# Wide cross-attention with its 64-channel heads: the given weights in place of folded ones

## The reference, cut to what matters

```python
xn, latn = _layernorm(x, ln1_w, ln1_b), _layernorm(latents, ln2_w, ln2_b)
q = latn @ Wq                                     # 16 heads of 64 channels
k, v = jnp.split(jnp.concatenate([xn, latn], axis=1) @ Wkv, 2, axis=-1)
...
weight = jax.nn.softmax(jnp.einsum('bhld,bhnd->bhln', q * scale, k * scale), axis=-1)
out = jnp.einsum('bhln,bhnd->bhld', weight, v)
return out.transpose(0, 2, 1, 3).reshape(b, l, INNER) @ Wo
```

## Time and profile before

| | us |
|---|---|
| median of 3 runs (2155.71 to 2158.64) | 2157.29 |
| the profiled execution, span | 2153.9 |
| PE busy | 1989.9 |
| DVE busy | 1582.0 |
| ACT busy | 1349.8 |
| POOL busy | 1015.9 |

### The profile page before, as it was taken

The page is one execution under the profiler, slowest core; times in us unless marked ns, Lnnn a source line. Parts: engine busy times, 40 slices in busy tenths (PEclk is TensorE's granted clock), DMA queues, the critical chain, the costliest instruction groups (busy, mean ns, idle before and its releaser), DMA issues.

```text
span 2153.9 us, 44630 instructions
## 1 busy us (share of the span) xinstructions
PE 1989.9 (92%) x14787; PEld 1692.3 (79%) x14849; DVE 1582.0 (73%) x3470; ACT 1349.8 (63%) x3140; POOL 1015.9 (47%) x1222
## 2 busy tenths in 40 slices
PE   6999989999999999998049999999999999999998
PEld 4787789999999999984047888887677777777776
DVE  5668568888888888777775666676787777788775
ACT  4666556666666666666774666787655555555554
POOL 3555444444454445420003655554356666566665
PEclk9999999999999999998568999999899999999999
DMA  6433400000000000000004444455233333333342
GB/s 182 122 118 119 112 1 2 1 1 2 1 2 1 2 1 2 1 1 1 0 3 130 118 119 115 122 163 158 81 118 120 121 125 118 120 120 122 120 126 97
DMA packets 138908, 161.03 MB, mean 75 GB/s; under 512 B 15340, under 2 KB 99244, under 8 KB 138284
## 3 DMA queue, kind: packets, MB, share of 16 engines
q1 hardware_dynamic: 132524, 153.46, 23.9%
q10 hardware_dynamic: 6160, 4.78, 0.7%
HBM read 119.75 MB, written 38.70 MB: 74 GB/s over the span
## 4 chain that ended last, share of the span: by engine, by line
PE 67%; issue 9%; POOL 8%; DVE 5%; ACT 5%; SPq 3%; DMA 2%; ACTq 0%; POOLq 0%; DVEq 0%
PE bank L947 8%; POOL h_lo L2122 7%; PE bank L273 6%; PE bank L911 5%; PE bank L913 5%; PE bank L912 5%; PE bank L1777 5%; PE bank L958 5%; PE bank L1779 5%; PE bank L1778 5%; PE bank L284 3%; PE bank L255 3%; PE bank L1680 2%; PE bank L254 2%; SPq L191 1%
## 5 line engine op out<-in xcount | busy, mean ns | idle before, releaser
L2122 POOL TENSOR_TENSOR h_lo<-h,h_hi 128x512 fp32r<-128x512 f32 x264 | 341.2, 1293 | 244.7 <-ACT h_hi L1903 244.6
L1304 POOL TENSOR_TENSOR pw<-ew,rw 128x410 f32<-128x410 f32 x256 | 225.6, 881 | 368.2 <-DVE rw L1166 351.5
L556 DVE TENSOR_REDUCE nmx<-bank 128x4 fp32r<-128x512 f32 (+1 forms) x384 | 237.6, 620 | 192.3 <-PE bank L255 189.0
L449 ACT ACTIVATE pt<-bank 128x512 f32<-128x512 f32 (+1 forms) x384 | 229.1, 600 | 128.2 <-PE bank L273 127.1
L1896 ACT ACTIVATE sl<-bank 128x512 f32<-128x512 f32 x264 | 157.8, 598 | 237.9 <-PE bank L1779 236.5
L1067 ACT ACTIVATE ew<-bank,nmax 128x205 f32<-128x205 f32 x512 | 216.8, 431 | 132.7 <-DVE nmax L1158 132.7
L2041 DVE TENSOR_TENSOR bank<-bank,sl 128x512 f32<-128x512 f32 x264 | 184.1, 697 | 142.1 <-PE bank L1779 114.1
L706 POOL TENSOR_SCALAR_AFFINE_SELECT pt<-pt 128x512 f32<-128x512 f32 x256 | 162.3, 635 | 187.7 <-ACT pt L449 187.6
L273 PE MATMUL bank<-q_pack,k_diag 128*128 128x128 f32 (+1 forms) x1536 | 237.8, 279 | 0.3
L273 PEld LDWEIGHTS bank<-q_pack,k_diag 128*128 128x128 f32 (+1 forms) x1536 | 189.1, 181 | 46.2 <-issue 37.9
L947 PE MATMUL bank<-kvt,qs 128*128 128x205 f32 x1024 | 221.6, 339 | 0.0
(11 more groups left out here) (349 smaller groups left out, 5215.8 us busy)
## 6 DMA issues: line engine op xcount, KB each, us to landing
share_b<-share_rows SPq DMA_DIRECT2D x256, 256.0 KB, 3.1
q_rows<-q_hi SPq DMA_DIRECT2D x96, 128.0 KB, 2.7
q_pack<-q_rows SPq DMA_DIRECT2D x32, 384.0 KB
raw<-in_experts SPq DMA_DIRECT2D x33, 192.0 KB, 3.2
q_rows<-q_lo SPq DMA_DIRECT2D x48, 128.0 KB, 2.8
k_diag<-k_rows SPq DMA_DIRECT2D x64, 96.0 KB
q_pack<-q_rows SPq DMA_DIRECT2D x31, 192.0 KB
k_diag<-k_rows SPq DMA_DIRECT2D x124, 48.0 KB
```

What stands on the lines that cost most here:

```text
L449: nc.scalar.activation(m.pt[0:a.keys, c, :, :].rearrange("p h t -> p (h t)"), m.flip[c % 2][0:a.keys, :], ACT.Exp).then_inc(s.exped.semaph ...
L556: nc.vector.tensor_reduce(m.nmx[:, b % 2, :, 0, c], m.score[c % 2][:, 0:HC * a.columns].rearrange("p (h k) -> p h k", h=HC)[:, :, 0:a.keys ...
L1304: nc.gpsimd.tensor_tensor(m.pw[:, k, :, 0:KW], m.ew[:, k, :, :], m.rw[:, k, :].unsqueeze(2).broadcast_to([128, 2, KW]), ALU.mult)\
L2122: nc.gpsimd.tensor_tensor(m.h_lo[:, k % 3, :], m.h[:, (k + u) % 2, :], m.h_hi[:, k % 3, :].bitcast(F32), ALU.subtract).then_inc(s.los, 1)
```

## The change

The stage now computes queries, keys and values with the given weights. The products of weights are gone, `wide_w` holds Wq, Wk, Wv, Wo (128 x 1024 each) and is split once into `wide_hi` and `wide_lo`, in sequences 9 to 17 of attention 0; its four loads are issued at sequences 4 to 7 (before: 24 and 25). A couple of heads (2 x 64 channels) now fills 128 partitions:
- `query` and `key` make a couple's queries (256 columns) and keys (412 columns) for both sequences of the pair, with three products each, in odd steps, three couples ahead. DVE copies the queries and scales them, ACT copies the keys.
- `value` makes one of eight tiles of values in even steps: the values of half of the heads for one sequence and one part of its keys (128 or 77 rows), three products of 512 columns; DVE copies them to `vs`.
- `scores` are two fp32 products over 64 rows each: head 0 on rows 0 to 63, head 1 on rows 64 to 127, each into a bank of its own. Bank 0 serves head 0 of every step.
- `weigh` is four fp32 products (two parts of the keys by two heads), with 64 columns of weights and 128 moving columns; head h writes partitions 64 h to 64 h + 63. The probabilities aren't split any more, `pwt_lo` is gone.
- `project_out` is three products of 256 columns in even steps, where there were six in odd ones.
- The step's order on PE is scores, then the products of even or odd steps, then the transposes, then the weighing. The transposes share one bank (`turned`), both couples' mixes share another.
- POOL no longer splits the inputs: `kv_hi`, `kv_lo` are gone, and the split of the transposed inputs is on ACT and DVE.
- The start of the stage changes with it: transposed inputs at sequences 28 and 29, three value tiles, three keys and three queries up to the gap behind the last sequence.

The core of the diff:

```diff
-    def weight_products(g):
-        left, right = (0, 1) if g < 4 else (2, 3)
-        wait(pe, s.weight_lows, g)
-        for k in range(4):
-            h = 4 * (g % 4) + k
-            last = nc.tensor.matmul(m.products[:, 128 * k:128 * k + 128], m.wide_w[:, h, left, :],
-                                    m.wide_w[:, h, right, :], start=True, stop=True)
-        last.then_inc(s.weight_products, 1)
-
...
+    def value(p, v, t, bank, queries_before):
+        half, k, part = t // 4, t // 2 % 2, t % 2
+        wait(pe, s.queries, queries_before)
+        wait(pe, s.values, TILES * p + t)
+        pe.wait_ge(s.inputs_lo, 2 * p + k + 1)
+        rows = PART_ROWS[part]
+        keys, columns = slice(128 * part, 128 * part + rows), slice(512 * half, 512 * half + 512)
+        in_parts(bank[0:rows, :], m.kvt_hi[:, v, k, keys], m.kvt_lo[:, v, k, keys],
+                 m.wide_hi[:, WV, columns], m.wide_lo[:, WV, columns]).then_inc(s.valued, 1)
+
+    def query(p, v, c, bank, values_before):
+        wait(pe, s.values, values_before)
         wait(pe, s.queries, XC * p + c)
-        if c == 0:
-            pe.wait_ge(s.inputs_lo, p + 1)
-        for h in range(2):
-            last = in_parts(m.ask[:, 256 * h:256 * h + 256].rearrange("p (k t) -> p k t", k=2),
-                            m.score_hi[:, 2 * c + h, :], m.score_lo[:, 2 * c + h, :],
-                            m.kvt_hi[:, v, :, :], m.kvt_lo[:, v, :, :])
-        last.then_inc(s.asked, 1)
+        heads = slice(128 * c, 128 * c + 128)
+        in_parts(bank[:, 0:256].rearrange("p (k t) -> p k t", k=2), m.wide_hi[:, WQ, heads], m.wide_lo[:, WQ, heads],
+                 m.kvt_hi[:, v, :, 0:T], m.kvt_lo[:, v, :, 0:T]).then_inc(s.asked, 1)
+
+    def key(p, v, c):
+        wait(pe, s.keys, XC * p + c)
+        pe.wait_ge(s.inputs_lo, 2 * p + 2)
+        heads = slice(128 * c, 128 * c + 128)
+        in_parts(m.key_bank[:, 0:2 * KP].rearrange("p (k t) -> p k t", k=2), m.wide_hi[:, WK, heads], m.wide_lo[:, WK, heads],
+                 m.kvt_hi[:, v, :, 0:KP], m.kvt_lo[:, v, :, 0:KP]).then_inc(s.keyed, 1)
 
     def scores(p, v, n):
         j, c, k = STEPS * p + n, n // 2, n % 2
         pe.wait_ge(s.queries, XC * p + c + 1)
+        pe.wait_ge(s.keys, XC * p + c + 1)
         wait(pe, s.exped, j - 1)
+        wait(pe, s.exped_first, j)
         for h in range(2):
-            last = nc.tensor.matmul(m.score[k][:, KP * h:KP * h + KW], m.qs[:, c % 2, h, k, :],
-                                    m.kvt[:, v, k, 0:KW], start=True, stop=True)
+            rows = slice(XD * h, XD * h + XD)
+            last = nc.tensor.matmul(score_bank(m, k, h)[:, 0:KW], m.qs[rows, c % 2, k, :],
+                                    m.ks[rows, c % 2, k, 0:KW], start=True, stop=True)
         last.then_inc(s.scores, 1)
 
...
     def transpose_probs(p, v, n):
         j, k = STEPS * p + n, n % 2
         pe.wait_ge(s.probs, j + 1)
-        wait(pe, s.prob_lows, j - 1)
+        wait(pe, s.probs_s, j)
         for part in range(2):
             for h in range(2):
                 at = 256 * part + 128 * h
-                last = nc.tensor.transpose(m.flip[k][:, at:at + 128],
-                                           m.pw[:, k, h, 128 * part:128 * part + 128], m.ident[:])
+                last = nc.tensor.transpose(m.turned[0:PART_ROWS[part], at:at + 128],
+                                           m.pw[:, k, h, 128 * part:128 * part + PART_ROWS[part]], m.ident[:])
         last.then_inc(s.probs_t, 1)
 
     def weigh(p, v, n):
-        j, c, k = STEPS * p + n, n // 2, n % 2
-        if n == 0:
-            pe.wait_ge(s.contexts, 2 * p + 2)
+        j, c, k, half = STEPS * p + n, n // 2, n % 2, n // XC
+        pe.wait_ge(s.values, TILES * p + 4 * half + 2 * k + 2)
         if k == 0:
-            wait(pe, s.head_lows, XC * p + c - 1)
-        pe.wait_ge(s.prob_lows, j + 1)
+            wait(pe, s.head_lows, XC * p + c)
+        pe.wait_ge(s.probs_s, j + 1)
+        at = 256 * (c % 2) + 128 * k
         for part in range(2):
-            keys = slice(256 * part, 256 * part + 256)
-            last = in_parts(m.mix[c % 2][:, 256 * k:256 * k + 256], m.kv_hi[:, v, k, part, :], m.kv_lo[:, v, k, part, :],
-                            m.pwt_hi[:, k, keys], m.pwt_lo[:, k, keys], part == 0, part == 1)
+            rows = PART_ROWS[part]
+            for h in range(2):
+                head, probs = XD * (n // 2 % 4 * 2 + h), 256 * part + 128 * h
+                last = nc.tensor.matmul(m.mix[XD * h:XD * h + XD, at:at + 128], m.vs[0:rows, half, k, part, head:head + XD],
+                                        m.pwt[0:rows, k, probs:probs + 128], start=part == 0, stop=part == 1)
         last.then_inc(s.weighted, 1)
 
     def project_out(p, v, c):
         if c == 0:
             wait(pe, s.out_s, p)
         pe.wait_ge(s.head_lows, XC * p + c + 1)
-        for h in range(2):
-            last = in_parts(m.out[:, 0:256].rearrange("p (k t) -> p k t", k=2),
-                            m.out_hi[:, 2 * c + h, :], m.out_lo[:, 2 * c + h, :],
-                            m.us_hi[:, c % 2, :, h, :], m.us_lo[:, c % 2, :, h, :],
-                            first=c == 0 and h == 0, last=c == XC - 1 and h == 1)
-        last.then_inc(s.projected_out, 1)
-
-    def transpose_output(p, asked):
+        heads = slice(128 * c, 128 * c + 128)
+        in_parts(m.out[:, 0:256].rearrange("p (k t) -> p k t", k=2), m.wide_hi[:, WO, heads], m.wide_lo[:, WO, heads],
+                 m.us_hi[:, c % 2, :, :], m.us_lo[:, c % 2, :, :],
+                 first=c == 0, last=c == XC - 1).then_inc(s.projected_out, 1)
+
...
+    def even_step(p, v, n):
+        coupled = min(XC * p + n // 2 + AHEAD, XC * PAIRS)
+        if n == 4 and pair_exists(p - 1):
+            wait(pe, s.keys, coupled)
+            transpose_output(p - 1)
+        if n in (6, 8) and pair_exists(p + 1):
+            wait(pe, s.keys, coupled)
+            transpose_inputs(p + 1, 1 - v, (n - 6) // 2, m.key_bank)
+        if (p, n) == (0, 4):
+            pe.wait_ge(first.updated.semaphore, B)
+        if pair_exists(tile_of(p, n)[0]):
+            value(*tile_of(p, n), ask_bank(m, p, n), coupled)
+        if n >= 4:
+            project_out(p, v, n // 2 - 2)
+        elif pair_exists(p - 1):
+            project_out(p - 1, 1 - v, n // 2 + XC - 2)
+
+    def odd_step(p, v, n):
+        couple = couple_after(p, v, n // 2 + AHEAD)
+        if not pair_exists(couple[0]):
+            return
+        if n == 5:
+            wait(pe, s.updated, p)
+        if n in (7, 9) and pair_exists(p + 1):
+            pe.wait_ge(s.inputs_lo, 2 * p + 2 + (n - 5) // 2)
+        key(*couple)
+        query(*couple, ask_bank(m, p, n), min(TILES * p + AHEAD + n // 2 + 1, TILES * PAIRS))
 
     def body(p, v):
         for n in range(STEPS):
-            c, k = n // 2, n % 2
-            transpose_probs(p, v, n)
             if pair_exists(after(p, v, n + 2)[0]):
                 scores(*after(p, v, n + 2))
+            if n % 2 == 0:
+                even_step(p, v, n)
+            else:
+                odd_step(p, v, n)
+            transpose_probs(p, v, n)
             if pair_exists(after(p, v, n - 1)[0]):
                 weigh(*after(p, v, n - 1))
-            if n == 4:
-                wait(pe, s.updated, p)
-            if (p, n) == (0, 3):
-                pe.wait_ge(first.updated.semaphore, B)
-            if n in (8, 10) and pair_exists(p + 1):
-                pe.wait_ge(s.inputs_t, 2 * p + 3 + (n - 8) // 2)
-            if k == 0 and c + 2 < XC:
-                ask(p, v, c + 2)
-            elif k == 0 and pair_exists(p + 1):
-                ask(p + 1, 1 - v, c + 2 - XC)
-            if k == 1 and c > 0:
-                project_out(p, v, c - 1)
-            elif k == 1 and pair_exists(p - 1):
-                project_out(p - 1, 1 - v, XC - 1)
-            if n == 3 and pair_exists(p - 1):
-                transpose_output(p - 1, XC * p + 4)
-            if n in (7, 9) and pair_exists(p + 1):
-                transpose_inputs(p + 1, 1 - v, (n - 7) // 2, XC * p + (n - 7) // 2 + 6)
 
...
+    def copy_keys(p, v, c):
+        act.wait_ge(s.keyed, XC * p + c + 1)
+        wait(act, s.scores, STEPS * p + 2 * c - 2)
+        nc.scalar.copy(m.ks[:, c % 2, :, :].rearrange("p k t -> p (k t)"), m.key_bank[:, 0:2 * KP]).then_inc(s.keys, 1)
 
     def exponentials(p, v, n):
         j, k = STEPS * p + n, n % 2
         act.wait_ge(s.maxed, j + 1)
         wait(act, s.probs, j - 1)
         for h in range(2):
-            last = nc.scalar.activation(m.ew[:, k, h, :], m.score[k][:, KP * h:KP * h + KW],
-                                        ACT.Exp, bias=m.nmax[:, k, h:h + 1],
-                                        accum_out=m.sums[:, k, h:h + 1])
-        last.then_inc(s.exped, 1)
+            nc.scalar.activation(m.ew[:, k, h, :], score_bank(m, k, h)[:, 0:KW],
+                                 ACT.Exp, bias=m.nmax[:, k, h:h + 1],
```

(36 more changed lines are left out.)

334 lines of the change are left out of this document (170 added, 164 removed).

## The result

The changed kernel takes 2184.06 us (median of 4 runs, 2179.06 to 2187.71), the kernel before 2156.5 us beside it (4 runs, 2153.81 to 2158.64). The ratio is 1.0129, with a 95% interval from 1.0109 to 1.015: slower. The forecast was 2189 us, range 2120 to 2250. The profiled execution spans 2177.3 us, against 2153.9 before: +23.4 us on the span. It was the fastest of the four, 6.8 us under their median.

The account below looks back on a forecast made before the run. PE's own instruction stream was taken as the bound. Couples +50, early pairs -11 and stage start -7 gave +32 us: span 2186, or 2189 us on the median's scale, range 2120 to 2250.

Parts of the forecast that it names:

- Price of a mode change: PE, each wide-stage step: three array emptyings 0.30 us plus bare first weight loads 0.25, together 0.55 us a step.
- The sign that the prediction named: PE profile after the change: 0.20 us from the last start before a mode change to the next load, three times a step.
- Price of a score record: PE, wide stage: each score record takes 0.172 us, derived from the remainder of the old step.
- A couple: PE, two wide-stage steps: 5.49 us after the change against 5.10, +0.39 us, over 128 couples +50 us.
- Row halves side by side: PE scores: both heads' 64-row products run in parallel, 0.69 us a couple instead of 1.38.
- the rival at 2277: PE scores: the two 64-row halves do not run side by side, +88 us; chance 0.12.
- Column-half loads hidden: PE weighing: only the first 64-column load is bare (0.05 us); later loads hide, 0.44 us of products a step.
- The rival at 2227: PE weighing: loads stay bare in each of four depths, three more of 0.05 us a step, +38; chance 0.07 shared.
- waits a, b, c: New PE waits, all met: scores for an exponential, transposes for the `turned` copy, even weighing for `us_lo` (tightest, 0.4 us).
- Wait (b): PE transposes wait for the previous step's copy (0.59 us) from one-bank `turned`; it has over 1.5 us, so is met.
- Early pairs: First seven pairs' 12.8 us excess: reduced DVE work and longer steps return most, -11 us (between -5 and -12.8).
- Into the stage: Start of the wide stage: weight products and the `kvt_lo` wait go, new projections come; -7 us, bounds -12 and 0.

Follow-up runs that it names:

- the grouped version: Changed kernel with both steps of a couple issuing scores together and weighings together, halving array-mode changes; 2138.24 us, ratio 0.9906 to the kernel before.

## Why the prediction was right, point by point

- **What bounds.** PE, before and after; its waits in the stage are 2.3 us. Right.
- **Price of a mode change.** 0.55 us a step predicted, 0.52 measured by taking all three away. Right, and it decides the sign. The sign that the prediction named is in the trace: 0.20, 0.20 and 0.26 us from the last start before each change to the next load, the last one behind score records of 0.17 us.
- **Price of a score record.** 0.172 us. The prediction had it as what was left of a step, so that its sum of 2.55 us against 2.54 measured was no check of it. The kernel without mode changes is one: 0.69 us for four.
- **A couple.** 5.49 us predicted; 5.50 for the couple shown, and 0.364 us more than before by the eight steady pairs, where I had 0.39. The 0.026 us on 120 couples is 3 us.
- **Row halves side by side.** Right (twice as deep costs +0.348 us a step); the rival at 2277 is excluded. The Trainium skill's statement in "TensorEngine Tiling (Array Packing)", Key Properties, that different tiles multiply in parallel, agrees with this case's trace.
- **Column-half loads hidden.** The weighing region is 0.59 us, four depths of 0.11 and 0.15 for one change; three bare loads more would make it 0.74. In the trace the loads of the second depth start at 624.62, under the first products (624.56). The rival at 2227 is excluded. The rule in the Trainium skill, "TensorE: Matmul & The Clock Gate", Part 3, that a load overlaps running products only where the row group differs, does not hold here: all column halves use all rows.
- **The other engines (waits a, b, c).** All three were met: 1.9 us in two places for `ew`, both behind the table loads, nothing for `turned` or `us_lo` from 300 to 970 us. Wait (b) came up only in the grouped version.
- **Early pairs.** -11 predicted; the excess went from 12.8 to 2.5 us, -10.3. The size was right by luck, the reason wrong: the step "what DVE gives up returns most of it" fails, since DVE given back the same work loses 1.4 us, and the kernel before, with its norm steps elsewhere, gets 9.4 back. The rest of the excess was ACT's table loads, which the prediction doesn't have.
- **Into the stage.** -7 predicted, -8.2 measured at the third step. The 2.12 us for `kvt_lo` are gone, as predicted. The 2.45 for `pw` were to stay and are gone too, and 1.98 us for `ew` at 274.58 came instead: that the two nearly cancel is luck.
- **The end.** Nothing predicted; the last pair's rest and the tail gave 1.9 us, where by 0.39 us a couple I had counted some 3 us of loss for the last pair. No keys, values or queries are left to compute there, so those steps hold less work.

The forecast's span of 2186 was 9 us too high: 3 from the couples, 5 from the last pair and the tail, 1 from the start, and almost 1 the other way from the early pairs. On the scale of the median it was only 5 us too high (2189 against 2184.06), because the profiled execution was a fast one of its kernel: that part of the closeness is chance.

## What to carry over

Count the changes of array mode in a loop, not only the columns that pass: at 0.16 to 0.17 us each they can cost more than the arithmetic that half-array products save; so gather the products of one mode from several steps. After such a grouping look again at the engine that got its work in one burst. And when an engine delays another, ask what stands directly ahead of the instruction that is waited for before asking how busy the engine is: norm steps of 0.8 to 0.9 us, moved by one step, gave back 9.4 us of the stage, with the same work.

## What was not expected of the hardware

- PE lost time in the early pairs of the kernel before that the view of waits hardly shows. The norm steps cost 9.4 us, and the view has 1.5 us for `qs` and 0.3 for `pwt_lo`; its 3.0 us for `pw` follow the table loads. In the timeline of PE, one step behind the wait for `qs` at 393.52:

```profile
395.54 0.28 PE L913 MATMUL bank<-pwt_hi,kv_lo 128*128 128x256 f32 x1
395.81 0.39 PE L911 MATMUL bank<-kvt_hi,score_hi 128*128 128x256 f32 x1
396.03 0.28 PE L912 MATMUL bank<-kvt_lo,score_hi 128*128 128x256 f32 x1
```

  The starts lie 0.27 and 0.22 us apart where 0.12 is usual, and no wait is listed, as a record still runs. A wait as short as the record ahead of it disappears in the busy time, and takes a bare load of 0.10 us with it. Starts show it, waits don't.
- The grouped kernel's runs spread by 20 us (2126.74 to 2147.09), and the mean granted clock of a run goes with them: 0.965 in the fastest, 0.954 in the slowest. In its profiled execution the clock is 1.00 in the stage from 290 to 620 us and lower elsewhere, in a part of the later stages that this work never touched (0.91 from 1500 to 1700 us; the changed kernel, which is there 46 us later, has 0.97 from 1546 to 1746). What sets it off stays open. The 11 us between the grouped kernel's median and its best go with this clock; that they come from it alone is not shown.
